# Two VectorE scalars moved ahead of two butterflies in the loop of a Hadamard-quantized FFN kernel

## The reference, cut to what matters

```python
# x: [64, 64, 512], one row of itok per sample, 200 sets of 64x64 weights
w = weights[conditions]
h0 = einsum('bct,bcd->bdt', x, w)                # [64, 64, 512]

def act_quant(x, bits=8):                        # per token (last axis)
    scale = 127 / clip(max(abs(x), axis=-1), 1e-5)
    return clip(round(x * scale), -127, 127) / scale

def weight_quant(w):                             # ternary, one scale
    scale = 1 / clip(mean(abs(w)), 1e-5)
    return clip(round(w * scale), -1, 1) / scale

def hbitlinear(x, w):                            # fwht: Walsh-Hadamard transform
    return einsum('bsd,fd->bsf', act_quant(fwht(x)), weight_quant(w))

h = hbitlinear(h0, w_up)                         # 512 -> 1024
h = square(relu(h))
out = x + hbitlinear(h, w_down)                  # 1024 -> 512
```

## Time and profile before

| | us |
|---|---|
| median of three runs | 261.35 |
| profiled execution | 261.15 |
| its span | 259.0 |
| TensorE matmul busy | 247.2 (95%) |
| TensorE weight load busy | 206.9 (80%) |
| VectorE busy | 212.6 (82%) |
| GpSimd busy | 187.4 (72%) |
| ScalarE busy | 147.5 (57%) |

### The profile page before, as it was taken

One profiled execution on the slowest core, in us unless ns is written; L12 is line 12 of the kernel. 1 busy time (PEld: TensorE's weight loads), 2 busy tenths in 40 slices (PEclk: granted clock), 3 DMA queues, 4 the chain that ended last, 5 costly groups with the idle time before them and its releaser, 6 DMA issues. The chain is left out here.

```text
span 259.0 us, 6500 instructions
## 1 busy us (share of the span) xinstructions
PE 247.2 (95%) x1964; PEld 206.9 (80%) x1964; DVE 212.6 (82%) x391; ACT 147.5 (57%) x211; POOL 187.4 (72%) x231
## 2 busy tenths in 40 slices
PE   6999998999999899999999999999999999999884
PEld 6999998989888687887879787887878778777551
DVE  0589799979888996987969796997969989698992
ACT  0559994665764464573737375472827574753340
POOL 2124729396887899898979899897979585959520
PEclk9999999999999999999999999999999999999999
DMA  5897236437565965632648453451835264545424
GB/s 191 279 345 246 55 91 92 101 80 168 69 165 110 272 142 53 162 87 45 165 124 221 113 134 82 111 135 29 222 84 122 42 95 123 140 82 136 79 83 162
DMA packets 62632, 33.90 MB, mean 131 GB/s; under 512 B 52754, under 2 KB 52882, under 8 KB 62610
## 3 DMA queue, kind: packets, MB, share of 16 engines
q10 hardware_dynamic: 47856, 13.74, 28.6%
q1 hardware_dynamic: 14754, 19.90, 23.6%
HBM read 13.70 MB, written 8.39 MB: 85 GB/s over the span
## 5 line engine op out<-in xcount | busy, mean ns | idle before, releaser
L473 POOL TENSOR_TENSOR p<-g 128x512 f32<-128x512 f32 x60 | 74.9, 1282 | 21.0 <-DVE g L1206 20.4
L922 PE MATMUL h_ps<-zqT,w_upT 128*128 128x256 f16 x512 | 63.7, 273 | 0.9 <-DMA zqT<-zq 0.8
L943 PEld LDWEIGHTS u_ps<-had_sb,p 128*128 128x128 f32 x480 | 56.7, 192 | 6.8 <-issue 4.4
L943 PE MATMUL u_ps<-had_sb,p 128*128 128x128 f32 x480 | 59.2, 277 | 2.3 <-ACT uq L649 2.1
L649 ACT ACTIVATE uq<-u_ps,u_mul 128x1024 f16<-128x1024 f32 x30 | 33.4, 1112 | 44.8 <-DVE u_mul L1251 44.8
L922 PEld LDWEIGHTS h_ps<-zqT,w_upT 128*128 128x128 f16 x512 | 49.5, 98 | 10.1 <-DMA zqT<-zq 1.3
L965 PE MATMUL o_ps<-w_downT,uqT 128*128 128x512 f16 x232 | 54.8, 379 | 1.2 <-DVE out_sb L1257 1.2
L436 POOL TENSOR_TENSOR x_half<-x_all 128x512 f32 (+1 forms) x30 | 37.6, 1271 | 19.8 <-DMA x_all<-in_x_dram 16.2
L630 ACT ACTIVATE g<-h_ps 128x512 f32<-128x512 f32 x64 | 36.1, 595 | 20.5 <-PE h_ps L922 11.4
L1238 DVE TENSOR_REDUCE u_max<-u_ps 128x1 f32<-128x1024 f32 x30 | 36.5, 1217 | 4.8 <-PE u_ps L943 4.6
L965 PEld LDWEIGHTS o_ps<-w_downT,uqT 128*128 128x128 f16 x232 | 22.6, 98 | 22.3 <-issue 1.3
(11 more groups left out here) (75 smaller groups left out, 221.0 us busy)
## 6 DMA issues: line engine op xcount, KB each, us to landing
x_all<-in_x_dram SPq DMA_DIRECT2D x32, 256.0 KB, 3.4
out_dram<-out_sb SPq DMA_DIRECT2D x32, 256.0 KB, 2.1
w_raw<-in_L_ffn_w_up_dram ACTq DMA_DIRECT2D x4, 512.0 KB, 4.2
w_raw<-in_L_ffn_w_down_dram SPq DMA_DIRECT2D x4, 512.0 KB, 5.4
w_diag<-in_L_cond_weights_dram SPq DMA_DIRECT2D x62, 16.0 KB, 2.3
uqT<-uq ACTq DMA_TRANSPOSE x30, 3.1
zqT<-zq ACTq DMA_TRANSPOSE x14, 3.1
had_sb<-in_hadamard_dram ACTq DMA_DIRECT2D x1, 64.0 KB, 2.0
```

The costliest lines, as they stand in the source:

```text
L473: nc.gpsimd.tensor_tensor(new[:, :, m, :], old[:, :, 0, :], old[:, :, 1, :], (ALU.add, ALU.subtract)[m]).then_inc(s_p8[k], 1)
L922: mm = nc.tensor.matmul(h_all[:, u % 2, i, :], w_upT[:, q, f * P:(f + 1) * P], zqT[par][:, :, q, :], start=(q == 0), stop=(q == TC - 1))
L943: mm = nc.tensor.matmul(u_bank(t, k)[:, c * P:(c + 1) * P], p8[par][:, c, k * P:(k + 1) * P], had_sb[:, :], start=True, stop=True)
```

## The change

In `step` of VectorE's order, and there alone, `u_absmax(5,1)`, `u_floor(5,1)` and `u_invert(5,1)` now stand together, directly behind `residual(6,1)`. Behind them come `y_outer(0,0)` (two instructions), then `z_absmax(1,1)`, `z_floor(1,1)` and `z_invert(1,1)`. No instruction is added or taken away, and every wait stays with its instruction.

```diff
                 run(residual, 6, 1)
+                run(u_absmax, 5, 1)
+                run(u_floor, 5, 1)
+                run(u_invert, 5, 1)
                 run(y_outer, 0, 0)
-                run(u_absmax, 5, 1)
                 run(z_absmax, 1, 1)
                 run(z_floor, 1, 1)
-                run(u_floor, 5, 1)
-                run(u_invert, 5, 1)
                 run(z_invert, 1, 1)
```

## The result

The changed kernel takes 258.61 us (median of four runs, 258.08 to 260.0), the kernel before 261.4 beside it (260.92 to 261.57): ratio 0.990, 95% interval 0.9878 to 0.9922. It is 2.8 us faster, where 3.2 were forecast. Two later sets of six runs of the changed kernel, on two chips and each beside its own runs of the kernel before, gave 258.92 against 262.06 (0.989) and 258.13 against 261.54 (0.986): 3.1 and 3.4 us. The title speaks of two scalars; what moved are three instructions, the absmax with its floor and inverse.

The account below looks back on a forecast made before the run. TensorE's pace was taken to bound the kernel nearly everywhere. 7 x 0.45 = 3.15 us plus 0.08 makes 3.23 off 261.15, 257.95; with 0.2 for the median, 258.1 us, 8-in-10 range 256.9 to 259.6.

Parts of the forecast that it names:

- The wait that goes: In the loop, had_u of k = 0 waits for ScalarE's uq; 0.51 us a step, 0.45 of it to be gained.
- Little over a third of u_mul's lead reaches TensorE: In the loop's step, u_mul comes 1.36 us sooner, but uq follows y_split, so TensorE gains 0.45 us.
- What is late for it: On VectorE, y butterfly and z scalars come later, z's inverse and g_outer by up to 0.35 us; quant_z covered by 0.3.
- The loop's count: Seven loop steps from 99.00 to 201.94 us give 7 x 0.45 = 3.15 us.
- the eighth wait: Placed in finish's first had_u; at most 0.16 us of its 0.45 is kept, 0.08 taken.
- `finish`: Behind the loop, VectorE isn't sooner relative to the step, so 0.08 us of the last 0.45 is kept.
- The rival of the back jump: At the loop's three jumps, a stall of 0.41 us replaces the wait; gain only 2.0 us, 259.35; chance 0.12.
- The rival of the full gain: In the loop the whole wait goes, cold start included: 8 x 0.51 = 4.1 us, 257.2; chance 0.06.
- The rival of no change: Within the step the wait moves to had_z, waiting for zq: 261.3 us; chance 0.07.
- The rival of GpSimd: Later g_outer delays GpSimd's x_outer, so project waits 0.60 us a step; 1.2 us slower, 262.55; chance 0.05.

Follow-up runs that it names:

- second and third profiles: Profiles of the changed kernel run again unaltered, in two later sets: 258.92 us against 262.06, and 258.13 against 261.54.
- floor-and-inverse half alone: Kernel before with u_floor and u_invert directly behind u_absmax, y_outer staying ahead of the absmax: 259.03 us, ratio 0.9905.
- absmax's place alone: Kernel before with u_absmax ahead of y_outer, u_floor and u_invert staying behind z_floor: 261.87 us against 262.06, ratio 0.9993.
- ScalarE's order changed: Changed kernel with quant_u ahead of y_split in ScalarE's step: 258.03 us, ratio 0.9856.
- large memset: Changed kernel with an unread 128x1280 memset ahead of x_outer in GpSimd's step: 262.51 us against 261.8, ratio 1.0022.
- `finish` edit: Changed kernel with u_floor and u_invert of tile 11 directly behind their absmax in finish, ahead of g_inner: 258.09 us against 261.8, ratio 0.985.
- dose of 0.52: Changed kernel with an unread 128x512 memset ahead of x_outer in GpSimd's step: 258.51 us.

## Why the prediction was right, point by point

- **The wait that goes.** `had_u` of `k = 0` behind `uq` was the one large wait of the loop, and it went whole. Step length: 14.2 to 14.3 us forecast, 14.25 measured in the second and third profiles, 14.29 in the first.
- **Little over a third of u_mul's lead reaches TensorE.** `u_mul` was to come 1.36 us sooner, and `uq` 0.45, for it follows `y_split`. Counted from the step's `had_u` they came 1.36 and 0.42 sooner. The floor-and-inverse half alone shows that it is so: 0.70 us of lead bring the same as 1.36. The absmax's place alone fits: moved by 0.66 us with `u_mul` standing still, it brings nothing. The gap from `y_split` to `uq` was taken from another place of ScalarE's timeline at 0.28, and it is 0.28. That `y_split` and TensorE's own matmuls allow `had_u` at nearly the same time (142.65 and 142.67 in the prediction) is a coincidence of this kernel. The changed kernel's time can't tell the two limits apart; the run with ScalarE's order changed shows that with `y_split` out of the way only 0.06 us a step is left to win.
- **What is late for it.** z's inverse was priced at up to 0.35 us later. Counted from the step's `down` it was at 11.42 (130.30 to 141.72) and is at 11.75 (130.08 to 141.83). `g_outer` went from 11.99 to 12.31. VectorE's wait ahead of `residual` was forecast at some 1.2 us and is 8.2/7 = 1.17. The reserve was real, and `quant_z` had its cover.
- **The loop's count.** The seven steps were to give 7 x 0.45 = 3.15; they gave 3.19 and 3.22 in the later profiles and 2.91 in the first. There one step took 14.57, with its `had_z` waiting for `zq` behind a transpose that took 1.52 us to issue. My text put the eighth wait in the wrong place: the first `had_u` of `finish` is already the seventh of the window, and the eighth stands ahead of step 9. It went too: from `had_u` of `k = 1` in step 8 it is 6.62 us to step 9 before (92.38 to 99.00) and 6.19 after, 0.43 sooner. The sum comes out the same, since it counted eight gains and gave most of one back. In the second profile the parts are 0.43 ahead of step 9 and 3.19 in the loop, less 0.24 by the longer wait for `x_half` in step 8 and 0.42 in `finish`: 2.96, and the span is 2.9 us shorter.
- **`finish`.** It was to give back 0.37 of a step's gain, VectorE not being sooner there in relation to TensorE. The second `had_u` of `finish` stands 6.57 us behind the first in place of 6.23, so 0.34 back, and 0.07 behind it, because it had to wait. What I had not seen is the long issue of the transpose, and this is the term that was missing. From that `had_u` to the one of tile 12 it is 5.26 us before, and 5.34, 5.54 and 5.70 in the three profiles, where the issue takes 1.83, 2.14 and 2.31. The kernel with the large memset has the same wait and an issue of 1.25, and needs 5.33. So an issue of 1.83 costs nothing yet, and the two longer ones 0.2 and 0.4. The `finish` edit takes out both the wait and the long issue.
- **The rival of the back jump.** VectorE shows its 0.4 us still, and `had_u` of TensorE none, at any of the three. My text has the rival hold at every jump by the rule that it cites. That was read too widely: the Trainium skill (Runtime: NRT & Kernel Launch, "Instruction fetch mechanics") predicts a stall only when the target isn't at hand, and TensorE's rows show none at the jump. What I overlooked is smaller and comes later. The three steps that follow a jump are 0.09 to 0.10 us longer than the others (14.30 against 14.21 in the second profile), and there `zq` of `k = 0` is 0.15 us later and the weight loads of `had_z` wait 0.16 us for it. These are the three waits for `zq` of the earlier trace rows. The kernel before has the same (14.76 against 14.66), so the gain isn't touched. That the jump is what makes `zq` late was not tried.
- **The rival of the full gain.** The cold start remained. ScalarE's order takes it away, 0.06 us a step.
- **The rival of no change.** `zq` and `had_z` did move along with TensorE: `zq` of `k = 0` starts 9.77 or 9.92 us behind the step's `had_u` in the second profile, 9.78 or 9.94 before, in most steps.
- **The rival of GpSimd.** Its idle time fell from 0.99 to 0.54 us a step, as much as TensorE's gain. In the traced step `x_outer`'s first part ends at 145.75 + 1.25 = 147.00 and `project` starts at 147.81: 0.8 us to spare, where 0.58 were forecast. A dose of 0.52 is free in these steps and one of 1.16 costs 0.32 a step.

What the later `g_outer` did to GpSimd shows in the step ahead of the traced one. Its short `u_deq` took 1.22 us at 127.38 before, beside the `g_outer` that had begun at 127.32, and 0.19 at 127.62 after, for that `g_outer` now begins at 127.96. The `z_now` behind it went from 1.19 to 0.19 us as well. In exchange the two `up_unit` behind them take 2.54 in place of 0.54 us. Whole instructions changed places, and the sum stayed: 2.95 before, 2.92 after. With the Trainium skill's exclusive lock (SBUF — State Buffer, "SBUF: two separate sides") these rows agree; the loss that I had drawn from it as a rival didn't come.

## What to carry to other kernels

Follow a wait back through every engine's order, not only through the data: what a scale that is ready sooner brings is capped by whatever stands ahead of its reader, and by the work that stands ahead of the wait itself. Here a third of the lead was worth everything. Order the scalars of a chain by who waits for them; a dependent chain's gaps may lie open on an engine that has idle time later in the same step. And look at what follows the loop: the order there was fitted to the old timing and gave back some 0.2%.

## What the runs showed of the hardware that was not expected

A DMA transpose takes ScalarE's queue 1.25 us to issue. In `finish` of the kernels with the faster loop it takes 1.83 to 2.38 us, unless their `finish` was edited or the large memset is in, and ScalarE starts nothing that stands behind it meanwhile. The trace's record of the DMA packets has one 16 KB instruction fetch there (the page's queue q8), and its time fits:

```
                    transpose issue          fetch
before              206.96 to 208.22         207.92 to 208.88
absmax's place      207.32 to 208.57         208.27 to 209.84
changed, first      205.32 to 207.63         205.72 to 207.15
changed, second     204.17 to 206.00         204.57 to 205.56
changed, third      204.28 to 206.42         204.69 to 205.96
large memset        207.75 to 209.00         203.89 to 204.84
finish edit         203.34 to 204.59         205.31 to 206.27
```

Where the fetch begins 0.4 us into the issue, the issue lasts until 0.4 to 0.5 us after the fetch has ended; where the issue is nearly or wholly done by then, it takes 1.25. In the kernel before, with the absmax's place and in the changed kernel, the fetch falls 5.97 us behind the first `had_u` of `finish`; with the `finish` edit, which issues the transpose ahead of it, 6.53. So making the loop faster moved the transpose, not the fetch, against that `had_u`: it is issued 5.02 us behind it in the kernel before and 5.57 in the changed one.

The large memset comes close to a test of it. Its `finish` is the changed kernel's, and the transpose stands at the same place, 5.57 us behind the first `had_u`, but the fetch falls 1.71 us behind it, and the issue takes 1.25 us.

With ScalarE's order changed, another transpose met a fetch, at the loop's start: issued from 98.00 to 100.30, fetch from 98.65 to 99.80. All issues above 1.8 us in these profiles have a fetch in them. Some of 1.37 to 1.53 us have none, such as the one of 1.52 in the loop of the first profile, so a fetch isn't all that can lengthen an issue. That a fetch holds it up is still read from such times: it was not tried alone, and the trace doesn't name the engine that fetches.

The second thing is small: with the wait gone, `had_u` still started cold, with 1.85 us to the next run in place of 1.79, where `uq` ended 0.15 us ahead of its start (142.32 and 142.47). Where `uq` ended 0.69 us ahead of it (ScalarE's order changed, 140.09 and 140.78), it didn't.
